# Probabilities of two half-chunks transposed as one packed strip, and attention side work dealt anew over eight units

## The reference, cut to what matters

```
h   = layernorm(x)
q   = h @ Wq.T + bq ; k, v = ctx @ Wk.T + bk, ctx @ Wv.T + bv     # 16 heads of 16
p   = softmax(where(mask == 0, -1e9, q @ k.T / 4))                # [256, 77] per head
x   = x + (p @ v) @ Wo.T + bo
h2  = layernorm(x)
x   = x + shared(h2) + expert(h2)      # shared: silu(h2 Wg) * (h2 Wu) @ Wd, width 512
                                       # expert: 1 of 16 per token, scaled by sigmoid(logit)
```

## Time and profile before

| | |
|---|---|
| median of 3 runs | 392.1 us (390.1 to 392.56) |
| profiled execution, its own time | 395.31 us |
| its span, first to last instruction | 393.3 us |
| mean granted TensorE clock | 0.98 of full |
| TensorE busy | 352.2 us (90%) |
| VectorE busy | 191.6 us (49%) |
| ScalarE busy | 172.9 us (44%) |
| GpSimd busy | 159.5 us (41%) |

### The profile page before, as it was taken

How to read it: one execution, slowest core, us unless ns; L and a number is a source line. 1 busy time by engine, 2 the same in 40 slices (tenths; PEclk the granted TensorE clock), 3 DMA queues, 4 the chain that set the end, 5 groups by cost and what they waited for, 6 DMA issues and landing times.

```text
span 393.3 us, 9350 instructions
## 1 busy us (share of the span) xinstructions
PE 352.2 (90%) x3068; PEld 225.3 (57%) x3068; DVE 191.6 (49%) x567; ACT 172.9 (44%) x472; POOL 159.5 (41%) x271
## 2 busy tenths in 40 slices
PE   2778788999999999998999999979998999999780
PEld 1556466777777777776776888424443434444330
DVE  2479899967967949767742852112121212111110
ACT  1258979665665565756641311312333232332310
POOL 5354656433522623422221021333656464656411
PEclk9989999999999999999999999989999999999987
DMA  8330102020069300000014999384558696314940
GB/s 239 145 85 3 44 0 72 0 72 2 27 231 408 125 0 27 27 26 3 27 55 168 397 273 363 114 343 147 184 163 287 223 350 209 106 41 159 380 197 20
DMA packets 23326, 56.47 MB, mean 144 GB/s; under 512 B 7275, under 2 KB 14461, under 8 KB 19968
## 3 DMA queue, kind: packets, MB, share of 16 engines
q1 hardware_dynamic: 16704, 48.59, 34.6%
q0 software_dynamic: 2880, 6.31, 5.0%
q10 hardware_dynamic: 3712, 1.22, 1.3%
HBM read 149.94 MB, written 6.82 MB: 399 GB/s over the span
## 4 chain that ended last, share of the span: by engine, by line
PE 30%; issue 27%; POOL 16%; DVE 13%; ACT 5%; DMA 5%; POOLq 1%; DVEq 0%; ACTq 0%
PE ps L651 8%; POOL xs L504 5%; POOL attT L512 5%; PE ps L657 5%; PE ps L578 4%; PE ps L593 3%; DMA rows<-score 3%; POOL pool_carrier L493 3%; POOL out L519 2%; PE ps L632 2%; DVE arena L1127 2%; PE ps L603 2%; ACT arena L935 2%; DVE den L1136 2%; DMA mask_in<-mask 2%
## 5 line engine op out<-in xcount | busy, mean ns | idle before, releaser
L451 POOL TENSOR_TENSOR arena<-arena,rden 128x308 f32<-128x308 f32 x64 | 44.7, 699 | 95.0 <-DVE rden L1140 94.3
L935 ACT ACTIVATE arena<-arena,negtop 128x77 f32<-128x77 f32 x256 | 70.6, 350 | 19.2 <-DVE negtop L1132 19.2
L1356 DVE TENSOR_TENSOR act_g<-act_g,ps 128x512 f32<-128x512 f32 x20 | 13.8, 688 | 90.9 <-PE ps L862 90.9
L493 POOL TENSOR_TENSOR pool_carrier<-neghalf 1x1 f32<-1x1 f32 x60 | 11.0, 183 | 81.2 <-DVE qT L1363 48.3
L603 PE MATMUL ps<-ident,arena 128*77 128x128 f32 x256 | 40.4, 284 | 2.1 <-ACT arena L943 2.1
L862 PE MATMUL ps<-own,qT 128*32 128x512 f32 x320 | 37.9, 615 | 4.4 <-DMA own<-w_experts 3.5
L862 PE MATMUL ps<-arena,qT 128*32 128x512 f32 x320 | 38.1, 617 | 3.8 <-DMA arena<-w_experts 3.6
L651 PE MATMUL ps<-xn2T,w_gu 128*128 (+1 forms) x160 | 39.5, 390 | 0.6 <-ACT xn2T L948 0.6
L603 PEld LDWEIGHTS ps<-ident,arena 128*77 128x77 f32 x256 | 30.0, 150 | 10.6 <-issue 6.7
L651 PEld LDWEIGHTS ps<-xn2T,w_gu 128*128 128x128 f32 x160 | 28.8, 189 | 10.0 <-issue 5.9
L1035 ACT ACTIVATE qT<-ps 128x256 f32<-128x256 f32 x20 | 7.7, 383 | 59.5 <-PE ps L851 59.5
(11 more groups left out here) (149 smaller groups left out, 579.2 us busy)
## 6 DMA issues: line engine op xcount, KB each, us to landing
own<-w_experts SPq DMA_DIRECT2D x44, 1024.0 KB
arena<-w_experts SPq DMA_DIRECT2D x44, 1024.0 KB
own<-w_experts SPq DMA_DIRECT2D x44, 512.0 KB
arena<-w_experts SPq DMA_DIRECT2D x44, 512.0 KB
arena<-x SPq DMA_DIRECT2D x8, 256.0 KB, 3.1
rows<-xn_now SPq DMA_DIRECT2D x7, 256.0 KB, 2.7
base<-x SPq DMA_DIRECT2D x5, 256.0 KB, 2.1
arena<-w_qkvoT SPq DMA_DIRECT2D x4, 256.0 KB, 5.2
```

Of the source, the lines that this page charges most:

```text
L451: pool.tensor_tensor(prob[k][:, :, :], prob[k][:, :, :], rden[k][:, :].rearrange("p (h o) -> p h o", o=1).to_broadcast([P, HU, K]), ALU.mu ...
L493: pool.tensor_tensor(pool_carrier[:, i:i + 1], neghalf[0:1, 0:1], neghalf[0:1, 0:1], ALU.add).then_inc(parted[i], 1)
L935: ins = act.activation(prob[k][:, h, :], prob[k][:, h, :], ACT.Exp, bias=negtop[k][:, h:h + 1])
```

## The change

1. The two units of a pair lie side by side in one strip `pair` of 640 columns: 616 of probabilities and 24 zeros. `transpose_prob` transposes it in five chunks of 128 columns, two at the even unit and three at the odd one, so 5 transposes of 128 x 128 take the place of 8 of 128 x 77.
2. `read_probT` copies 128 x 256 at the even unit and 128 x 384 at the odd one, in place of 77 x 512 twice.
3. A chunk holds the keys of up to three heads, so `vz` gets a row for each of the 5 x 128 packed rows and 128 columns for each chunk of the width. `attend_pair` still makes 8 products (4 strips of 32 rows, 2 chunks each), now over 128 rows.
4. GpSimd's `place_values` goes; the sync engine's queue does it with 12 DMAs for each batch (a head's rows, cut at chunk borders), of 16 columns (64 bytes) in each element.
5. `cap` and `xnT` move from the arena to `spread`; `val` is doubled; the memset of `zeros` goes, that of `vz` grows from 512 to 1280 columns (twice), four small ones for the zeros of `pair` are new.
6. The side work is dealt anew. VectorE: unit 0 `ln1_stats` (now after the unit's own work) and `add_attention` (was unit 1), 3 `read_kv` (was 2), 4 `ln1_apply` (was 1), 5 `read_mask` (was 0) and `ln2_stats` (was in `add_attention`), 6 `ln2_apply` (was 3). GpSimd: 2 `rstd_first` (was 0), 3 `keep_residual` (was 2), 4 and 5 `spread_keys` (was 3, 4), 6 `rstd_second` (was 2). TensorE: X at the end of unit 4 (was 2), Q at the start of unit 6 (was 3), where it also waits for `early_h`. ScalarE: `read_xnT` at 5 (was 2), `read_q` at 6 (was 3).

```
-        vz = [carve(H * HG, K).rearrange("k (h d) -> k h d", h=H) for s in range(2)]
-        prob = [carve(HU * K).rearrange("p (h k) -> p h k", h=HU) for s in range(UB)]
+        vz = [carve(DC * NCH * P).rearrange("p (c j d) -> p c j d", c=DC, j=NCH) for s in range(2)]
+        pair = [carve(NCH * P) for s in range(UB // 2)]
+        prob = [pair[s // 2][:, (s % 2) * HU * K:(s % 2 + 1) * HU * K].rearrange("p (h k) -> p h k", h=HU) for s in range(UB)]
...
+            def place_values(b):
+
+                s = b % 2
+                sp.wait_ge(val_ready, b + 1)
+                if b == 0:
+                    sp.wait_ge(vz_zero, 2)
+                if b >= 2:
+                    sp.wait_ge(pv_done, UB // 2 * (b - 1))
+                for h, k, j, p, n in pieces:
+                    sp.dma_start(vz[s][p:p + n, :, j, h * HD:(h + 1) * HD],
+                                 val[s][k:k + n, :].rearrange("k (c d) -> k c d", c=DC)[:, :, h * HD:(h + 1) * HD]).then_inc(vals_in[s], 16)
 
             for b in range(B - 2):
                 sp.wait_ge(kv_psum, b + 1)
...
                 load_batch(b + 2)
+                place_values(b)
...
             def transpose_prob(q, s, k, started):
...
-                for h in range(HU):
-                    mm = pe.transpose(ps[0:K, bank_pt[k % 2], h * P:(h + 1) * P], prob[k][:, h, :], ident[:, :])
+                for j in (range(2, NCH) if k % 2 else range(2)):
+                    mm = pe.transpose(ps[:, bank_pt[k % 2], (j % 2 if j < 2 else j - 2) * P:(j % 2 + 1 if j < 2 else j - 1) * P],
+                                      pair[k // 2][:, j * P:(j + 1) * P], ident[:, :])
                 mm.then_inc(pt_psum, 1)
...
                 if k == 0:
-                    pe.wait_ge(vals_ready, b + 1)
+                    pe.wait_ge(vals_in[s], 16 * len(pieces) * (q + 1))
...
+                    for g in range(HC // 2):
+                        j = HG // HD * g * K // P + a
+                        mm = pe.matmul(ps[HG * g:HG * (g + 1), bank_o, c * S + t * P:c * S + (t + 1) * P],
+                                       vz[s][:, c, j, HG * g:HG * (g + 1)], probT[k // 2][:, j, :], start=(a == 0), stop=(a == 1))
...
                 if k == 4:
                     if not last:
-                        pe.wait_ge(q_out, DC * (b + 2))
+                        pe.wait_ge(val_ready, b + 2)
                     early_gate_up(g, 2, bank_m[0])
...
+                    if k == 6 and not last:
+                        if shared:
+                            pe.wait_ge(early_h, FC * (2 * q + (s - EARLY)) + 3)
+                        project_q(nq, ns, bank_m[0])
                     if k % 2 == 0 and n != 0:
                         attend_pair(*unit_at(q, s, k - V_LAG), n != 1)
...
+                lo, hi = (2, NCH) if k % 2 else (0, 2)
+                act.activation(probT[k // 2][:, lo:hi, :].rearrange("p j n -> p (j n)"), ps[:, bank_pt[k % 2], 0:(hi - lo) * P],
                                ACT.Copy).then_inc(pt_out, 1)
...
                     if k == 0 and not last:
-                        read_mask(nq, ns)
-                    if k == 1 and not last:
-                        ln1_apply(nq, ns, True)
-                    if k == 1 and n not in (0, 1):
+                        ln1_stats(nq, ns)
+                    if k == 0 and n not in (0, 1):
                         add_attention(q - 1, s)
-                    if k == 2 and not last:
-                        read_kv(nq, ns)
                     if k == 2 and shared:
                         early_hidden(q, s, 0, bank_f)
-                    if k == 3 and n not in (0, 1):
-                        ln2_apply(q - 1, s)
+                    if k == 3 and not last:
+                        read_kv(nq, ns)
                     if k == 4 and shared:
                         early_hidden(q, s, 1, bank_f)
+                    if k == 4 and not last:
+                        ln1_apply(nq, ns, True)
+                    if k == 5 and not last:
+                        read_mask(nq, ns)
+                    if k == 5 and n not in (0, 1):
+                        ln2_stats(q - 1, s)
                     if k == 5 and shared:
                         early_hidden(q, s, 2, bank_m[0])
                     if k == 6 and shared:
                         early_hidden(q, s, 3, bank_f)
+                    if k == 6 and n not in (0, 1):
+                        ln2_apply(q - 1, s)
```

More of the change, by code:

```diff
@@ L124, in xattn_moe @@
         mask_in = [sb(f"mask_in{s}", [P, QT, K], I32) for s in range(2)]
-        cap = [carve(QT * K).rearrange("p (t k) -> p t k", t=QT) for s in range(2)]
+        cap = [spread[:, UB // 4 * NCH * P + DC * S + s * QT * K:UB // 4 * NCH * P + DC * S + (s + 1) * QT * K].rearrange("p (t k) -> p t k", t=QT)
+               for s in range(2)]
         seen = sb("seen", [P, QT, K])
@@ L213, in xattn_moe @@
         xres_ready, seen_ready, cap_ready = sem("xres_ready"), sem("seen_ready"), sem("cap_ready")
-        vz_zero, val_ready, vals_ready = sem("vz_zero"), sem("val_ready"), sem("vals_ready")
+        vz_zero, val_ready, pad_zero = sem("vz_zero"), sem("val_ready"), sem("pad_zero")
+        vals_in = [sem(f"vals_in{s}") for s in range(2)]
         kv_psum, kv_out, kblk_ready = sem("kv_psum"), sem("kv_out"), sem("kblk_ready")
@@ L243, in xattn_moe @@
         parted = [sem(f"parted{i}") for i in range(3)]
+        pieces = []
+        for h in range(HC):
+            r = h * K
+            while r < (h + 1) * K:
+                end = min((h + 1) * K, (r // P + 1) * P)
+                pieces.append((h, r - h * K, r // P, r % P, end - r))
+                r = end
         block = ctx.enter_context(nc.Block())
@@ L404, in _ @@
                 pool.memset(digit[:, :, c, :], float(CODES ** c)).then_inc(const_ready, 1)
+            for a in range(UB // 2):
+                pool.memset(pair[a][:, PAIR:NCH * P], 0.0).then_inc(pad_zero, 1)
             for s in range(2):
-                pool.memset(vz[s][:, :, :], 0.0).then_inc(vz_zero, 1)
-            pool.wait_ge(zero_ready, 1)
+                pool.memset(vz[s][:, :, :, :], 0.0).then_inc(vz_zero, 1)
             pool.wait_ge(const_ready, 14 + NL)
@@ L435, in spread_keys @@
                                    ALU.mult).then_inc(kblk_ready, 1)
[L437 to L447, removed]
             def normalise(q, s, k):
@@ L465, in batch @@
                         continue
-                    if k == 1 and n == 0:
-                        place_values(0, 0, 0)
                     if k == 2:
+                        rstd_first(nq, ns)
+                    if k == 3:
                         keep_residual(nq, ns)
[L470 to L473, removed]
+                    if k in (4, 5):
+                        spread_keys(nq, ns, k - 4)
             rstd_first(0, 0)
@@ L598, in transpose_prob @@
                 u = UB * (2 * q + s) + k
+                if not started and k == 1:
+                    pe.wait_ge(pad_zero, UB // 2)
                 pe.wait_ge(normalised, u + 1)
@@ L969, in batch @@
                     exponential(q, s, k)
+                    if k == 5 and n != B - 1:
+                        read_xnT(nq, ns)
+                    if k == 6 and n != B - 1:
+                        read_q(nq, ns, bank_m[0])
                     if k == 1 and shared:
@@ L1105, in read_k, with read_v @@
                                       ALU.add).then_inc(kv_out, 1)
-            def read_v(bank, at):
-                dve.tensor_tensor(val[:, :], ps[0:K, bank, at:at + D], b_vo[0:K, 0, :], ALU.add).then_inc(val_ready, 1)
+            def read_v(s, bank, at):
+                dve.tensor_tensor(val[s][:, :], ps[0:K, bank, at:at + D], b_vo[0:K, 0, :], ALU.add).then_inc(val_ready, 1)
             def read_kv(q, s):
@@ L1113, in read_kv @@
                 dve.wait_ge(kblk_ready, DC * b)
-                dve.wait_ge(vals_ready, b)
+                if not isinstance(q, int) or q > 0:
+                    dve.wait_ge(vals_in[s], 16 * len(pieces) * q)
                 read_k()
-                read_v(bank_m[0], 2 * K)
+                read_v(s, bank_m[0], 2 * K)
             def mask_scores(q, s, k, started):
@@ L1193, in batch @@
                 for k in range(UB):
-                    if k == 0 and not last:
-                        ln1_stats(nq, ns)
                     if k >= S_LAG or n != 0:
@@ L1238, in _ @@
                 invert(q7, 1, k)
-            add_attention(q7, 0)
-            ln2_apply(q7, 0)
-            add_attention(q7, 1)
-            ln2_apply(q7, 1)
+            for s in range(2):
+                add_attention(q7, s)
+                ln2_stats(q7, s)
+                ln2_apply(q7, s)
             steps = [0]
```

43 lines of the change are left out of this document (20 added, 23 removed).

## The result

The changed kernel takes 401.51 us (median of 4 runs, 399.35 to 402.11) against 392.33 for the kernel before, run beside it (4 runs, 390.1 to 392.67): a ratio of 1.0236, 95% interval 1.0182 to 1.0291. I had forecast 389.0, and 401.5 lies above my range.

A forecast was written before the change was run, and what follows sets the result against it. TensorE was taken to set the pace from batch 3 on, VectorE in batch 2; -3.0 - 1.5 + 1.3 + 0.2 - 0.1 = -3.1 us against the median of 392.1 gave 389.0, bounds 386.5 to 391, overall range 383 to 395.

The forecast's parts named there:

- Together +0.2, bounds -1 and +2: Batches 0 and 1: batch 1 about 15.1 for 15.5, batch 0 making batch 1's first scores 0.6 late; +0.2 us in all.
- +1.3; bounds 0 and 2: Batch 2, paced by VectorE: side work moved to units 4 to 6 adds waits, 18.7 us for 17.40.
- Rival 4: More VectorE stalls: Q's wait at its upper bound, batch 2 at +2, batch 0 at lower clock; 391 to 395.5, chance 0.15.
- Middle batches: Batches 4 to 6: TensorE's savings less added waits give -1.0 us each, cycle near 26.2 for 27.20; -3.0 in all.
- the transposes': Packed transposes on TensorE: 0.25 us for two and 0.35 for three, 0.60 a pair; each pair saves 0.43.
- X in the open, +0.43: Middle batch, unit 4: X, formerly hidden in the wait before unit 3's score pair, now costs 0.43 us.
- The last batch: No X or Q to move; chains hold units 2, 3 and 6, G0 delayed by 0.4, pairs give it back: -0.1 us.
- prologue: Memsets ahead of `rstd_first` add about 1.5 us, covered by VectorE's wait for the mask until 8.98; otherwise they'd count.
- Rival 2: A transpose's time goes by its columns, 0.21 us each, so packing saves nothing: 394.5 us, chance 0.10.
- values by DMA: Twelve DMA issues and one landing take some 8 us, hidden in about 13 of slack for batch 0; no cost.
- Rival 3: Values come late: each DMA piece waiting for the previous landing makes `attend_pair` of batch 0 19 late; 411 or more, chance 0.07.
- rival 1: VectorE's waits don't bind: TensorE's whole gain gives 379.5 us, chance 0.10; half of it 383 to 386.5, chance 0.15.

The follow-up runs named there:

- e1_warm: The changed kernel with filler products on TensorE ahead of X and Q in batches 0 to 2: 394.99 us, ratio 1.0054 to the kernel before.
- e4_mixed: The changed kernel with the side work in its old places in batches 0 to 2, new places from batch 3 on: 391.4 us, ratio 0.9994.
- e3_deal_alone: The kernel before with only the new places of side work, keeping 77-column transposes and values placed by GpSimd: 401.06 us, ratio 1.0237.
- e5_early_x: e4_mixed with the first layernorm's apply at unit 1 and X at unit 2 from batch 3 on: 396.56 us on a slower chip, ratio 0.9966.

## Why the prediction was wrong, step by step

- **The step that failed** is "Together +0.2, bounds -1 and +2" for batches 0 and 1, with batch 2's "+1.3; bounds 0 and 2". Measured: +5.6 and +3.5. I priced every TensorE group there at its full-clock duration and let the clock in for batch 0 alone. Yet the very step that I worked out, X after `ln1_apply` at unit 4 and Q behind its copy, says that TensorE has almost nothing to do before Q in all three batches. The row that should have warned me was in the earlier trace rows: a mean clock of 0.95 over batches 0 and 1 before any change (cut apart, 0.89 in batch 0 and 1.00 in batch 1). Rival 4 named the mechanism ("batch 0 at the lower clock") and gave it 391 to 395.5, with the price of one batch.
- **Of the 9.2 us**, e1_warm gives back 2.8 in batch 1 and 1.5 in batch 2: 4.3 are the clock's by the traces. In batch 0 the run's slow first products (1.9) hide what it gave back; without them it would have taken 16.1 for 17.89, so I estimate 1.8 more, and 6.1 in all, near the 6.5 between the medians. The other 3.1 are there at full clock: batch 2 at 19.45 is +2.05, just over my bound, batch 1 at 16.35 is +0.8 (1.25 over my 15.1), batch 0 +0.3 by the same estimate, against a batch 0 of the kernel before that had itself lost about 1 to the clock. In batch 1 the late Q shows plainly: the pair of units 6 and 7 starts 11.1 after the batch's start for 12.5 before, but the next batch's first pair follows it by 5.25 for 3.0, with Q in between.
- **Middle batches**: waits as forecast (0.89 for 1.06, 0.31 for 0.25). The cycle came to 26.7 to 26.8 and not 26.2. The term mis-sized is the transposes': 0.27 and 0.42 start to start for two and three, 0.69 a pair, where I had 0.25 and 0.35. Three pairs lie outside unit 3's wait and make 0.27 of the missing 0.5. Q's wait is another 0.13: from gate-up 3's start to Q's start it is 2.30, for 1.92 from gate-up 3 to what follows it in the kernel before, so 0.38 and not 0.25. The small rest is spread over several groups. Batch 3 gained 0.9 for 1.5.
- **X in the open, +0.43** was right: moving X back into the wait gives 26.05 for 26.70, more than the 0.43, as Q comes 0.21 sooner after gate-up 3 (2.09 for 2.30).
- **The last batch** (-0.1) was right. The **prologue** (nothing) was right in this execution by luck: the power that `ln1_apply` needs came 1.2 later than before (6.98 for 5.76), and the mask had landed just late enough to cover that. In the eight other packed traces it landed earlier, and VectorE waits 0.36 (e4_mixed) to 0.92 (e1_warm) for the power. The condition "if that cover went, they'd count" was the right one.
- **Rival 2** (a transpose goes by its columns) is refuted: five take 0.76 busy, and eight of 77 columns take 1.10 in e3_deal_alone's middle batch. The weight loads of these transposes say the same: 147 ns on average at 77 columns (L603 of the kernel before) and 141 at 128 (L620 of the changed one). The Trainium skill's columns / 1.2 ns (TensorE: Matmul & The Clock Gate, "LDWEIGHTS (loading the stationary operand)") thus isn't met at 77 columns.
- **The values by DMA** cost nothing, as forecast, but with less slack than I thought. The sync engine's queue in batches 0 and 1, for one set of twelve and the loads behind it (start, time, count):

```profile
30.51 10.21 SPq L311 DMA_DIRECT2D arena<-val  x12
45.06 0.35 SPq L286 DMA_DIRECT2D ctx_in<-ctxT  x1
45.45 0.43 SPq L287 DMA_DIRECT2D arena<-x  x1
```

An issue takes 0.85, so twelve take 10.2, where I had put issues and landing together at some 8; with one landing (2.7) it is 12.9, about the 13 that I gave batch 0. No TensorE wait of the changed kernel names them.
- **Rival 3** (the values late) didn't come, and **rival 1** (TensorE's whole gain) neither: the wait at unit 3 is there in every middle batch.

## What to carry to other kernels

Where a stage keeps TensorE only partly busy, price its matmuls at both clock levels before moving work in it: a projection pushed behind two waits of 1 to 2 us took twice its time, and it stood on the path. Deal work by stage, since an order that suits batches with the shared layer spoiled those without. Put a movable piece of TensorE work into a wait that another chain sets (X at unit 2, 0.65 us a batch); faster transposes alone bought 0.17 of the 1.1 that they freed.

## What the runs showed of the hardware

- The fall of the clock differs between runs of one program. Batch 2 of the same instructions took 17.19, 17.21 and twice 18.84 us (mean granted clock 1.00 and 0.91). The Trainium skill, TensorE: Matmul & The Clock Gate, section "HAM oscillation — how this bites in real kernels", has waits for DMA between bursts of matmuls put the clock back to 1.2 GHz; the traces agree for waits on VectorE and ScalarE of 2.0 and 1.3 us with few products between, and add that one program falls on either side from run to run.
- The half rate can stand in the durations while the granted clock of the window still reads 1.00. In seven of the thirteen traces the first score pair of batch 0 takes 1.40 for 0.79, and the prologue's Q takes 3.75 at a record of 1.00 in the changed kernel too. The durations are the surer sign, and such a start makes batch 0 1.5 to 1.9 us longer (15.46 in e4_mixed, 13.95 in e5_early_x, the same program there).
- A DMA of 64-byte pieces within SBUF held the issuing queue for 0.85 us, against 0.33 to 0.48 for the loads of the context, the rows and the mask in the same stretch.
- A fp32 product of 128 x 128 x 128 costs 0.24 us of TensorE (18 records in 2.17), so nine of them fill a gap of two microseconds.
